# One layer's attention started from the norm ahead of it, and its batch loop written out

## The reference, cut to what matters

```
x: (32, 56, 128)   ctx_768: (32, 1500, 96)   16 heads of 8
def _L3_xattn_ref(query, key_value, Wq, bq, Wk, bk, Wv, bv, Wo, bo):
    q = (query @ Wq + bq) by heads
    k = (key_value @ Wk + bk) by heads
    v = (key_value @ Wv + bv) by heads
    attn = clip(q . k * 8 ** -0.5, -10000, 10000)
    attn = softmax(attn)
    attn = where(any(isnan(attn)), 1 / Nkv, attn)
    return (attn @ v) @ Wo + bo
...
x = x + tanh(g_xattn[3]) * _L3_xattn_ref(_layernorm(x), ctx_768, ...)
x = x + tanh(g_ffn[3]) * _L3_ffn_ref(_layernorm(x), ...)
```

## Time and profile before

| what | us |
|---|---|
| median of 3 runs | 4428.92 (4426.80 to 4431.22) |
| the profiled execution | 4428.97 |
| its span on the core | 4427.3 |

### The profile page before, as it was taken

One profiled execution on the slowest core, in us unless ns is written; L12 is line 12 of the kernel. 1 busy time (PEld: TensorE's weight loads), 2 busy tenths in 40 slices (PEclk: granted clock), 3 DMA queues, 4 the chain that ended last, 5 costly groups with the idle time before them and its releaser, 6 DMA issues. The chain is left out here.

```text
span 4427.3 us, 85895 instructions
## 1 busy us (share of the span) xinstructions
PE 3752.2 (85%) x33246; PEld 2490.9 (56%) x33246; DVE 2734.5 (62%) x3533; ACT 2056.9 (46%) x2955; POOL 1422.6 (32%) x1888
## 2 busy tenths in 40 slices
PE   7389999945379999998999997679867799989996
PEld 7267777723236666664666664257523366656663
DVE  8656666552255555525555553467554899989993
ACT  7167777711113334332433442166412477767762
POOL 0164545213422323212333220022101655656630
PEclk9689999967779999997999997889988799999997
DMA  6166767544232223212332320021000666666640
GB/s 170 47 149 162 172 165 171 127 157 176 68 73 73 82 81 86 77 45 72 86 88 77 85 76 24 9 64 47 5 17 20 149 156 152 149 140 152 155 105 15
DMA packets 197059, 434.56 MB, mean 98 GB/s; under 512 B 45707, under 2 KB 98877, under 8 KB 196588
## 3 DMA queue, kind: packets, MB, share of 16 engines
q1 hardware_dynamic: 122308, 339.44, 29.1%
q0 software_dynamic: 38912, 47.06, 5.0%
q10 hardware_dynamic: 35504, 43.39, 3.7%
HBM read 244.72 MB, written 32.67 MB: 63 GB/s over the span
## 5 line engine op out<-in xcount | busy, mean ns | idle before, releaser
L1471 DVE TENSOR_REDUCE L_mp<-ps 112x2 f32<-112x1000 f32 x384 | 458.2, 1198 | 508.1 <-PE ps L1293 504.6
L1330 PE MATMUL ps<-L_p,L_cn 125*97 125x448 f32 x1536 | 639.2, 538 | 0.0
L1454 ACT ACTIVATE L_p<-ps 125x896 f32<-125x896 f32 x384 | 352.2, 917 | 613.7 <-PE ps L1318 540.5
L2141 ACT ACTIVATE L_p<-L_p 125x896 f32<-125x896 f32 x384 | 364.7, 950 | 228.7 <-DVE L_p L2194 228.0
L2177 DVE TENSOR_REDUCE L_mp<-ps 112x2 f32<-112x1000 f32 x384 | 455.6, 1191 | 6.6 <-PE ps L1954 6.6
L2194 DVE SCALAR_TENSOR_TENSOR L_p<-ps,xn 125x896 f32<-125x896 f32 x384 | 414.8, 1082 | 41.0 <-PE ps L1973 30.0
L1316 PE MATMUL ps<-L_qh,L_ch 97*125 97x448 f32 x768 | 386.0, 503 | 14.0 <-DMA L_qh<-L_mc 14.0
L1330 PEld LDWEIGHTS ps<-L_p,L_cn 125*97 125x97 f32 x1536 | 250.4, 163 | 205.9 <-issue 165.9
L1954 PE MATMUL ps<-L_ks,L_qs 96*128 96x500 bf16 x768 | 236.3, 393 | 62.4 <-DVE L_mp L2177 50.7
L918 ACT ACTIVATE L_p<-ps,rk 125x896 f32<-125x896 f32 x256 | 257.5, 1007 | 68.0 <-PE ps L775 64.2
L1317 PE MATMUL ps<-L_ql,L_ch 96*125 96x448 f32 x768 | 284.5, 370 | 0.0
(11 more groups left out here) (531 smaller groups left out, 7446.8 us busy)
## 6 DMA issues: line engine op xcount, KB each, us to landing
L_ks<-L_k_part SPq DMA_DIRECT2D x288, 375.0 KB, 7.4
L_ks<-L_k_first SPq DMA_DIRECT2D x96, 375.0 KB, 6.2
moe_w<-in_L_w SPq DMA_DIRECT2D x64, 512.0 KB
L_cn<-in_ctxN SPq DMA_DIRECT2D x32, 568.4 KB
cs_ct<-in_ctxT SPq DMA_DIRECT2D x32, 562.5 KB, 4.2
L_raw<-in_ctxT SPq DMA_DIRECT2D x32, 562.5 KB
L_cr<-in_ctxT POOLq DMA_DIRECT2D x32, 562.5 KB, 4.7
L_ch<-in_ctxT POOLq DMA_DIRECT2D x32, 562.5 KB, 4.4
```

The costliest lines, as they stand in the source:

```text
L1330: mm = nc.tensor.matmul(U[:, a, :], CN[s][:, j, :], P[:, n % 2, a * HALF:(a + 1) * HALF], start=(j == 0), stop=(j == KT - 1))
L1454: nc.scalar.activation(two(P[:, n % 2, :]), SB[n % 2], ACT.Exp).then_inc(S["exped"].sem, 1)
L1471: nc.vector.tensor_reduce(mp[:, 2 * k:2 * k + 2], ps[0:TT, bank:bank + 2, 0:500], AX.X, ALU.max).then_inc(S["chunk_maxed"].sem, 1)
L2141: nc.scalar.activation(two(P[0:KP, n % 3, :]), two(P[0:KP, n % 3, :]), ACT.Exp).then_inc(S["exped"], 1)
```

## The change

- `layer_norm` takes `fills` (work for POOL) and `room` (two tiles instead of its own `xc` and `x2`, which are now the memory of `KS[2]` and `KS[3]`). The L3 norm's Block gets SP's six loads (with a wait for all of them) and POOL's four fills: the rows of ones in `CK` and `CV`, and the ones of `KS[0]` and `KS[1]`.
- The ones of `KS[2]` and `KS[3]` are written by POOL, after `place_queries(first + 2)` and before the batches.
- Queries are made, scaled and split by quarters of 448 columns. The first quarter comes first on PE and DVE; the other three are made after the keys of batch 0 and split after batch 0's third key parts.
- The three key chunks of batch 0 use banks 5, 6 and 7, so PE doesn't wait for ACT between them.
- Batch 0's key parts are placed one by one, as each is ready. Its queries are placed half by POOL and half by ACT.
- `turn(first)` comes one step earlier (n = 13).
- `batches` writes all 32 batches out.

```diff
-def layer_norm(core, src, dst, tag, finish=None, loads=None, gated=None, aside=None):
+def layer_norm(core, src, dst, tag, finish=None, loads=None, gated=None, aside=None, fills=None, room=None):
...
-        xc = core.sb(f"xc{tag}", [D, T], F32, ctx)
-        x2 = core.sb(f"x2{tag}", [D, T], F32, ctx)
+        xc, x2 = room or (core.sb(f"{n}{tag}", [D, T], F32, ctx) for n in ("xc", "x2"))
...
-                    nc.clear_and_free_semaphores([s.sem for s in done])
+                    if done:
+                        nc.clear_and_free_semaphores([s.sem for s in done])
+                    if fills:
+                        fills(pool)
...
     def batches(eng, body):
 
-        for r in range(8):
-            body(Eight(None, r))
-        with eng.Fori(1, 3) as turn:
-            for r in range(8):
-                body(Eight(turn, r))
-        for r in range(24, B):
+        for r in range(B):
             body(Eight(None, r))
...
+    def ones_in_keys(pool, n):
+        nc.gpsimd.memset(KS[n][0:96, PAIRS * NK:].bitcast(F32), 0.0).then_inc(S["keys_zeroed"], 1)
+        pool.wait_ge(S["keys_zeroed"], 2 * n + 1)
+        nc.gpsimd.memset(KS[n][96:128, :].bitcast(F32), TWO_ONES).then_inc(S["keys_zeroed"], 1)
+        pool.wait_ge(S["keys_zeroed"], 2 * n + 2)
+
+    def loads(sp):
+        for dst, name in ((WQ[:, :], "WqP"), (WK[:, :], "WkP"), (WVE[:, :], "WvE"), (WOE[:, :, :], "WoE")):
+            sp.dma_start(dst, d[f"{L}_{name}"]).then_inc(S["w_in"], 16)
+        load_keys(sp, first)
+        load_values(sp, first)
+        sp.wait_ge(S["w_in"], 64)
+        sp.wait_ge(S["ck_in"], 16)
+        sp.wait_ge(S["cv_in"], 16)
+
+    def fills(pool):
+        for t in (CK, CV):
+            nc.gpsimd.memset(t[DC:KA, :], 1.0).then_inc(S["ones_row"], 1)
+        pool.wait_ge(S["ones_row"], 2)
+        for n in range(2):
+            ones_in_keys(pool, n)
...
+    norm(loads, fills, [KS[n][:, 0:2 * T].bitcast(F32) for n in (2, 3)])
...
+            place_part(first, 0)
+            load_keys(sp, first + 1)
+            place_part(first, 1)
+            place_part(first, 2)
...
             split_keys(first + 2)
             place_queries(first + 2)
+            pool.wait_ge(S["keys_third"], 9)
+            for n in (2, 3):
+                ones_in_keys(pool, n)
             batches(pool, body)
...
             def score(b, n):
                 if n == 0:
+                    pe.wait_ge(S["keys_zeroed"], min(2 * b.r + 2, 8))
...
+            make_queries(0)
             for c in range(3):
-                if c:
-                    pe.wait_ge(S["keys_copied"], c)
                 make_keys(first, c)
-            pe.wait_ge(S["keys_copied"], 3)
+            for c in range(1, NCH):
+                make_queries(c)
+            pe.wait_ge(S["keys_copied"], 1)
...
             split_keys(first)
+            act.wait_ge(S["q_zeroed"], 4)
+            act.wait_ge(S["q_split"], 1)
+            place_half(act, first, 1, "q_first")
             for g in range(4):
                 copy_values(first, g)
...
-            for n, t in enumerate(KS):
-                link(nc.vector.memset(t[0:96, PAIRS * NK:].bitcast(F32), 0.0))
-                nc.vector.memset(t[96:128, :].bitcast(F32), TWO_ONES).then_inc(S["keys_zeroed"], 1)
-                if n == 0:
-                    make_parts()
+            scale_queries(0)
+            split_queries(0)
+            nc.vector.memset(ps[:, 4, :], 0.0).then_inc(S["sums_zeroed"], 1)
+            for c in range(1, NCH):
+                scale_queries(c)
+            dve.wait_ge(S["keys_third"], 3)
+            for c in range(1, NCH):
+                split_queries(c)
```

More of the change, by code:

```diff
@@ L1563, with attention_clipped @@
                 "u_copied", "sums_picked", "sums_widened", "sums_spread", "sums_copied", "sums_inverted", "u_normed", "seen", "projected", "out_copied"]
[L1566 removed]
+def attention_clipped(core, L, src, bo, scale, clip, csum, norm):
     nc, d, ps = core.nc, core.d, core.ps
@@ L1578, in attention_clipped @@
         with ExitStack() as ctx:
-            clipped_pass(core, L, S, src, bo, scale, clip, ok, ctx)
+            clipped_pass(core, L, S, src, bo, scale, clip, ok, ctx, norm)
         N = core.sb(f"{L}_N", [KA, H, D], F32, outer)
@@ L1612, in _, with clipped_pass @@
                                           ps[0:KA, 4 + g, :]).then_inc(copied.sem, 1)
-def clipped_pass(core, L, S, src, bo, scale, clip, ok, ctx):
+def clipped_pass(core, L, S, src, bo, scale, clip, ok, ctx, norm):
     nc, d, ps = core.nc, core.d, core.ps
@@ L1727, in used_earlier, with load_keys, load_values, place_half @@
                 return emptied(*misc(b, k))
+    first = Eight(None, 0)
+    def load_keys(sp, b):
+        if b.r:
+            sp.wait_ge(S["keys_made"], b.lin(3, 0))
+        sp.dma_start(CK[0:DC, :], context(b)).then_inc(S["ck_in"], 16)
+    def load_values(sp, b):
+        if b.r:
+            sp.wait_ge(S["values_made"], b.lin(4, 0))
+        sp.dma_start(CV[0:DC, :], context(b)).then_inc(S["cv_in"], 16)
+    def ones_in_keys(pool, n):
[17 more added lines that the diff above has]
+            ones_in_keys(pool, n)
+    def place_half(eng, b, j, placed):
+        for u, (_, part) in enumerate(PRODUCTS):
+            r0 = u + NPROD * DH * j
+            eng.dma_start(queries(b)[r0:r0 + NPROD * DH:NPROD, :, j, :],
+                          qparts[part][64 * j:64 * j + 64, b.lin(NQ, 0):b.lin(NQ, NQ)]
+                          ).then_inc(S[placed], 16)
+    def key_bank(b, c):
+        return ps[:, 5 if b.r else 5 + c, 0:500]
+    norm(loads, fills, [KS[n][:, 0:2 * T].bitcast(F32) for n in (2, 3)])
     with nc.Block() as block:
@@ L1787, in _ @@
         def _(pool):
-            for t in (CK, CV):
-                nc.gpsimd.memset(t[DC:KA, :], 1.0).then_inc(S["ones_row"], 1)
-            pool.wait_ge(S["ones_row"], 2)
             link = core.linker(pool, "pool")
@@ L1796, in place_queries @@
             def place_queries(b):
-                if b.turn is not None or b.r >= 4:
+                pool.wait_ge(S["q_split"], b.r // 8 + 1)
+                if b.r >= 4:
                     pool.wait_ge(S["scored"], b.lin(12, -36))
-                for u, (_, part) in enumerate(PRODUCTS):
-                    for j in range(2):
-                        r0 = u + NPROD * DH * j
-                        pool.dma_start(queries(b)[r0:r0 + NPROD * DH:NPROD, :, j, :],
-                                       qparts[part][64 * j:64 * j + 64, bass.ds(b.lin(NQ, 0), NQ)]
-                                       ).then_inc(S[f"q_in{b.r % 4}"], 16)
+                place_half(pool, b, 0, f"q_in{b.r % 4}")
+                if b.r:
+                    place_half(pool, b, 1, f"q_in{b.r % 4}")
             def rest_of_keys(b, c):
@@ L1881, in make_keys @@
                     pe.wait_ge(S["ck_in"], b.lin(16, 16))
-                nc.tensor.matmul(ps[:, 5, 0:500], WK[:, :], CK[:, columns(c)], start=True, stop=True
+                nc.tensor.matmul(key_bank(b, c), WK[:, :], CK[:, columns(c)], start=True, stop=True
                                  ).then_inc(S["keys_made"], 1)
@@ L2001, in body, with make_queries @@
                     fifth_bank(b, k)
-            first = Eight(None, 0)
-            pe.wait_ge(S["w_in"], 64)
-            for c in range(NCH):
-                mm = nc.tensor.matmul(ps[:, c, 0:CH], WQ[:, :], src[:, c * CH:(c + 1) * CH], start=True, stop=True)
-            mm.then_inc(S["q_made"], 1)
-            pe.wait_ge(S["ones_row"], 2)
+            def make_queries(c):
+                nc.tensor.matmul(ps[:, c, 0:CH], WQ[:, :], src[:, c * CH:(c + 1) * CH], start=True, stop=True
+                                 ).then_inc(S["q_made"], 1)
+            make_queries(0)
             for c in range(3):
-                if c:
-                    pe.wait_ge(S["keys_copied"], c)
                 make_keys(first, c)
-            pe.wait_ge(S["keys_copied"], 3)
+            for c in range(1, NCH):
+                make_queries(c)
+            pe.wait_ge(S["keys_copied"], 1)
             for g in range(4):
```

76 lines of the change are left out of this document (33 added, 43 removed).

## The result

The changed kernel takes **4400.93 us** (median of 4 runs, 4396.61 to 4401.76), the kernel before, run beside it, 4430.07 us (4426.80 to 4431.75). The ratio is 0.9933, with a 95% interval of 0.9916 to 0.9950: 29 us, or 0.7%, faster; a second set of runs gave 17 us (the end of the experiments). The profiled execution took 4401.76 us (span 4400.2), against 4428.97 (span 4427.3) before. The forecast was 4404.2, in a range of 4394 to 4419.

What follows compares the result with a forecast made beforehand. DVE was taken to pace the batches, leaving the stage's start and the hole at the backward jump to win. The sum 18.5 + 13.8 - 7.5 = 24.8 us took 4428.97 to 4404.2, range 4394 to 4419.

Steps and rivals of the forecast that it cites:

- norm with loads and constant rows, extra: In the norm's Block of 16.7 us: SP's loads and POOL's fills both fit and cost nothing, 0 to 2 us allowed.
- six transfers on ACT: ACT's issues of batch 0's queries, ahead of the value copies: 3.6 us, from 2 to 30, priced like POOL's 0.56 each.
- first clip (T): DVE's first clip, before which the batches can't run: moves from 3485.81 to 3467.3.
- won at the start: The chain from the norm to DVE's first clip: 18.5 us earlier, with bounds of 14 to 24.
- given back by the memsets: POOL's two large memsets between the queries of batches 2 and 3 delay batch 1's maxima: 7.5 us, from 4 to 12.5.
- won by the loop: At the backward jump, the period of 40.03 us becomes 26.27 with the loop written out: 13.8 us won.
- behind the last reduction: From the last batch's once-a-batch reduction to the end: taken as unchanged, with no term in the sum.
- The sum of the bounds: Start 14 to 24, memsets 4 to 12.5, norm 0 to 2, taken together as 4395 to 4414 us.
- far from 3.6 us: Sign in the changed trace: the forecast is wrong if ACT's six issues take far from 3.6 us.
- rival of slow transfers: ACT's six issues take 5.03 us each, the chain gets 26.6 us longer, time 4430.8; chance 0.05.
- The rival that they cost nothing: POOL's two large memsets delay nothing if PE and ACT don't need POOL before T + 19: 4396.7 us; chance 0.08.
- The rival of a lasting low clock: PE stays at 1.2 GHz after batch 0's stop and paces the batches, 22 us more for each; chance 0.04.

Runs made afterwards that it cites:

- x1: The kernel before with only the loop over the 32 batches written out; median 4410.85 us, ratio 0.9971 to the kernel before.
- x2: The changed kernel with the loop of two turns put back and all else kept; median 4417.21 us, ratio 0.9980 to the kernel before.
- x12: The changed kernel with the steps behind the norm in old order, batch 0's query transfers all on POOL; 4402.36 us, ratio 0.9949 to the kernel before.
- x4: The changed kernel with all twelve of batch 0's query transfers issued by POOL, none by ACT; 4399.03 us, ratio 0.9936 to the kernel before.
- x3: The changed kernel with POOL's memsets of KS[2] and KS[3] moved right after batch 0's maxima parts; 4395.18 us, ratio 0.9929 to the kernel before.
- x11: Changed kernel with batch 0's queries on POOL, batch 2's keys sooner, memsets later, batch 3's query transfers behind its key steps; 4377.46 us, ratio 0.9892 to before.
- x5: The changed kernel with batch 0's maxima sent ahead of batch 3's load in SP's queue; 4400.49 us, ratio 0.9941 to the kernel before.
- x8: The changed kernel with the six loads of weights and batch 0's context put back behind the norm; 4418.28 us, ratio 0.9981 to the kernel before.

## Why the prediction was right, step by step

| step | predicted | measured |
|---|---|---|
| norm with loads and constant rows, extra | 0 (0 to 2) | 0 (16.7 us long as before) |
| first copy of batch 0's keys | 3399.9 | 3398.08 |
| six transfers on ACT | 3.6 | 6.49 |
| first value copy | 3409.9 | 3410.53 |
| first score | 3426.2 | 3426.58 |
| first score of batch 1 | 3445.6 | 3445.87 |
| first clip (T) | 3467.3 | 3468.04 |
| won at the start | 18.5 | 17.8 |
| given back by the memsets | 7.5 | 7.5 |
| won by the loop | 13.8 | 14.3 |
| behind the last reduction | 0 | 2.5 |
| sum | 24.8 | 27.1 (27.2 between the two profiled times) |

**The time.** The forecast of 4404.2 lies between the two medians of the changed kernel, 4400.93 and 4407.94. The sum of the bounds has a slip: 4414 leaves out the norm's 2 us, with which it is 4415.7. It changes nothing.

**The loop** went as predicted, and x1 and x2 show that it stands by itself. The half us beyond 13.8 is from the batches at the start of each turn of the loop (26.46 us where others take 26.2 or 26.3).

**The loads** cost the norm nothing, and all of the gain at the start is theirs and the constant rows': x12 with only these has a first clip 2.1 us sooner than the changed kernel. The prediction followed the chain as a whole and gave no share to the new order; by x4 and x12 it is worth 4.0 us, and the six issues on ACT that come with it take 6.1.

**The six transfers on ACT** were sized wrong: 6.49 us, or 1.08 each on average, not the 0.56 of POOL's issue of the same shape. By its own sign ("far from 3.6 us") this part of the forecast was wrong. This hardly shows in T, because other steps went the other way: PE ran the first quarter and the keys at the full clock (0.99 us, and 2.68 for three key chunks) where I had put the low one, which brought the first key copy 1.8 us sooner. The two errors cancelled to 0.7 us, which is luck. The range of 2 to 30 us held it, and the rival of slow transfers needed 4.7 us each to eat the gain. x4 shows that these issues lie on the path one to one, as the prediction had it.

**The memsets** went as described, and here too the size of 7.5 came by luck, from two errors that cancel. The period with the stop is 8.7 us too long (34.89 less 26.2), because PE stood for 7.92 us, not 6.5. Against this stand 1.2 us: from the first clip to maxima 1 it took 10.3 us instead of 11.5, as the clock recovered sooner. x3 then took the whole stop away with the memsets. They took 5.10 us each beside a busy DVE, as in the first layer. The rival that they cost nothing is wrong.

**PE at the low clock**: it was back at 1.00 in the stretch from 3500 on, and all periods from the third on are plain. The rival of a lasting low clock has fallen, too.

**What failed** is a term that the sum doesn't have: the stretch behind the last reduction, which I took as unchanged because its instructions are. It is 2.5 us shorter: 1.55 by a dip of the clock that this kernel doesn't have, most of the rest with a low stretch of 41.0 us instead of 44.4.

## What to carry to other kernels

When a transfer, a memset or a load is moved, look at what is queued behind it on its engine until the next thing that another engine waits for: in this start each of the waits that x3 to x11 removed was the issue order of one queue, no engine was full, and the reordered kernel (x11) is 24 us faster than the changed one by the marks. Removing one such wait brings what lies until the next, and that can be nothing (x5), so follow the chain past the place of the edit, and look for the second latest input as well. Written-out code is worth trying where a loop of few, long turns jumps back while all engines are busy: the one jump cost 14 us here.

## What the runs showed of the hardware

- An issue of a transfer by ACT took 1.08 us on average (6.49 for six, 7.21 in x8) where POOL's issue of the same shape takes 0.56. The six are not alike: in the changed kernel they took 1.26, 0.63, 0.62, 0.68, 1.68 and 1.47 us. SP was issuing its own transfers beside the first five. The Trainium skill (Perfetto Trace Analysis, its part on hardware-generated DMA instructions) says that the time shown includes the wait for a descriptor generator that two queues share. The trace agrees only in part: three issues were short beside SP's, and the sixth took 1.47 us after SP's last had ended at 3408.72, with only POOL still issuing. What holds the long ones is open; no run here had ACT issue alone.
- A TensorE that had idled for 14 us took 1.86 and 4.74 us for what else takes 0.99 and 2.68. The same start, in the kernel before and in x1, had its first clip 3.4 us apart; the largest single piece of this is 1.5 us at the query product (6.25 and 4.75 us), because the clock rose at another moment.
- POOL's memsets took 5.10 us each beside a busy DVE, but a small DVE instruction that usually takes 0.17 us (L_mc, from SBUF to SBUF) and began inside one ended only with it: it took 0.99 us in the changed kernel (until 3479.56, the memset until 3479.53), 3.44 in x5 and 0.90 in x11. In x5 the clip behind it took 3.36 us instead of 1.09. The clips and reductions that began inside a memset in the changed kernel took as long as ever (1.09 and 1.20 us).
- The same instructions at the end of the stage took 126.8 to 129.5 us in different kernels, and 126.77 and 126.76 in two profiles of the same one.
